# A four-layer attention and FFN kernel: weights folded inside the first chunk, first maxima inside the last one, and another arrangement of banks in the attention loop

## The reference

```python
scores = jnp.einsum('bhtd,bhtjd->bhtj', q, k_mod) * scale + pos_bias.T[None, :, None, :]
attn = jax.nn.softmax(jnp.where(valid[None, None], scores, jnp.finfo(scores.dtype).min), axis=-1)
out = jnp.einsum('bhtj,bhtjd->bhtd', attn, v_g) * if_gain[None, :, None, None]
...
h1 = jnp.einsum('gmh,goh->gmo', xg, W1) + b1[:, None, :]
h2 = jnp.einsum('gmo,gho->gmh', h1, W2) + b2[:, None, :]
...
attn = jax.nn.softmax(jnp.einsum('bqhd,bkhd->bhqk', q, k) * scale, axis=-1)
out = jnp.einsum('bhqk,bkhd->bqhd', attn, v)
```

## Time and profile before

| | |
|---|---|
| median of 3 runs | 2613.07 us (2612.34 to 2616.65) |
| profiled execution, its own time | 2615.01 us |
| its span, first to last instruction | 2613.2 us |
| PE busy | 2406.7 us (92%) |
| DVE busy | 2038.7 us (78%) |
| ACT busy | 1468.8 us (56%) |
| POOL busy | 727.3 us (28%) |
| granted PE clock, mean | 0.957 |

### The profile page before, as it was taken

One profiled execution on the slowest core, in us unless ns is written; L12 is line 12 of the kernel. 1 busy time (PEld: TensorE's weight loads), 2 busy tenths in 40 slices (PEclk: granted clock), 3 DMA queues, 4 the chain that ended last, 5 costly groups with the idle time before them and its releaser, 6 DMA issues. The chain is left out here.

```text
span 2613.2 us, 49018 instructions
## 1 busy us (share of the span) xinstructions
PE 2406.7 (92%) x15112; PEld 939.8 (36%) x15112; DVE 2038.7 (78%) x2445; ACT 1468.8 (56%) x2704; POOL 727.3 (28%) x936
## 2 busy tenths in 40 slices
PE   9688999999997648999999999999999999999678
PEld 7234455455445302323333333333333333333144
DVE  5388999999996348888888888888888888888145
ACT  0133444444434104777777777777777777777610
POOL 0688787787773033002002011020000000000110
PEclk9789999999998757999999999999999999999989
DMA  8334444554455197004004013031000000000161
GB/s 286 97 80 112 117 132 125 142 137 114 121 139 147 56 156 85 6 10 59 4 11 61 3 30 41 3 52 19 4 19 4 10 11 4 11 12 3 44 166 40
DMA packets 244668, 174.70 MB, mean 67 GB/s; under 512 B 105804, under 2 KB 215508, under 8 KB 244564
## 3 DMA queue, kind: packets, MB, share of 16 engines
q1 hardware_dynamic: 213048, 116.06, 16.9%
q0 software_dynamic: 13216, 36.72, 9.4%
q10 hardware_dynamic: 18304, 20.59, 2.7%
HBM read 116.49 MB, written 48.05 MB: 63 GB/s over the span
## 5 line engine op out<-in xcount | busy, mean ns | idle before, releaser
L1167 DVE TENSOR_REDUCE mx<-ps_m 128x1 f32<-128x1024 f32 x1036 | 1219.9, 1219 | 253.2 <-PE ps_m L1043 246.7
L1151 ACT ACTIVATE pr<-ps_s 128x512 f32<-128x512 f32 x2048 | 1114.9, 598 | 409.8 <-PE ps_s L1072 385.4
L1072 PE MATMUL ps_s<-qs,ks 99*128 (+1 forms) x2048 | 702.3, 382 | 9.9 <-ACT pr L1151 4.3
L1043 PE MATMUL ps_m<-ks,qs 96*128 (+1 forms) x2072 | 637.7, 389 | 39.9 <-DMA qs<-q_d 33.5
L1081 PE MATMUL ps_o<-pr,vg 128*32 128x512 f32 x4096 | 545.5, 605 | 0.2
L564 POOL TENSOR_TENSOR prod_p<-qT,kT 128x512 f32<-128x512 f32 x336 | 414.0, 1262 | 106.4 <-PE PSa L607 85.4
L1072 PEld LDWEIGHTS ps_s<-qs,ks 99*128 (+1 forms) x2048 | 195.8, 96 | 641.9 <-issue 441.0
L1000 POOL DMA_DIRECT2D vg<-vb_d x24 | 19.8, 824 | 1166.9 <-PE ps_o L1081 1166.5
L1043 PEld LDWEIGHTS ps_m<-ks,qs 96*128 (+1 forms) x2072 | 198.4, 98 | 252.3 <-issue 44.5
L815 DVE TENSOR_TENSOR prod_d<-PSa,kT 128x512 f32<-128x512 f32 x368 | 232.8, 678 | 25.0 <-PE PSa L607 15.5
L607 PE MATMUL PSa<-prod_p,sj 128*32 128x512 f32 x672 | 202.8, 617 | 10.0 <-DVE prod_d L815 7.5
(11 more groups left out here) (134 smaller groups left out, 2090.4 us busy)
## 6 DMA issues: line engine op xcount, KB each, us to landing
own<-skew SPq DMA_DIRECT2D x64, 512.0 KB
ks<-k_d POOLq DMA_DIRECT2D x42, 256.0 KB, 9.2
qs<-q_d POOLq DMA_DIRECT2D x168, 64.0 KB, 9.4
skew<-attn SPq DMA_DIRECT2D x64, 164.0 KB, 4.2
w<-in_W SPq DMA_DIRECT2D x32, 256.0 KB, 4.7
w<-in_W2T SPq DMA_DIRECT2D x32, 256.0 KB, 6.1
vb_d<-vb SPq DMA_DIRECT2D x8, 1024.0 KB, 5.3
q_d<-qparts ACTq DMA_DIRECT2D x16, 384.0 KB, 2.6
```

Of the source, the lines that this page charges most:

```text
L1043: mm = pe.matmul(ps_m[:, u % 2, kc * CH:(kc + 1) * CH], qs[0:KROWS, bass.ds(nq, 1), j, qt * P:(qt + 1) * P].rearrange("p a t -> p (a t)"), ...
L1072: pe.matmul(ps_s[:, op % SB, :], ks[:, bass.ds(slot, 1), j, kt * P:(kt + 1) * P].rearrange("p a t -> p (a t)"), qs[:, bass.ds(q, 1), j, :] ...
L1151: act.activation(pr[:, kt % 4, j, :], ps_s[:, op % SB, :], ACT.Exp, scale=HD ** -0.5).then_inc(p_ready, 1)
L1167: dve.tensor_reduce(mx[:, j * TILES + qt, half:half + 1], ps_m[:, u % 2, :], AX_X, ALU.max).then_inc(m_read, 1)
```

## The change

The change has three parts.

1. `fold_ffn` is gone. Its 32 pieces become steps `fold_load`, `fold` and `fold_out` of chunk 0 in the local stage, in a ring of four buffers, with the same matmuls and accumulation steps. One result buffer takes the place of two, and a second small matmul adds `b2`. The constants are loaded by ScalarE's queue.
2. The tensors of the full attention (`ks`, `qs` and others) are allocated ahead of both stages, and the local stage's big tensors are views of them. In chunk 7, behind the last product, GpSimd's queue loads the first keys and the queries of two chunks (18 transfers, `ahead_load`), and PE and VectorE make 88 maxima over 512 columns each (`ahead`), 64 for the first query chunk and 24 for the second. The attention's first pass of this kind is gone; at its start SP loads the queries of chunks 2 and 3.
3. In the attention loop the scores have four banks, the maxima three of one bank each; a `max_unit` is one matmul and a reduction over 512 columns, behind each score; values are made for two tiles at a time, once in eight scores. The transposed negative maxima use a maxima bank.

Beside these, the softmax of the local stage is made otherwise: the maximum's negative is the bias of eight exponentials on ScalarE, which also give the sums; the mask is added only for the first three tiles of a batch; the gain goes into `wo` once. `LEAD`, by which products are moved ahead, is 0.5 instead of 1.0, and the tables of positions are new.

```diff
+    (5.12, "fold_load", 19), (5.87, "fold_load", 20), (6.3, "fold_load", 21), (7.11, "fold_load", 22), (7.26, "load_v96", 0),
...
+            def fold(i):
+                g, r = i // PIECES, i % FOLD_RING
+                need(pe, fold_sb, g)
+                pe.wait_ge(fold_ld[r], 32 * (i // FOLD_RING + 1))
+                for m in range(KC):
+                    for k in range(FOLD_K):
+                        mm = pe.matmul(PS[:, TAIL_BANK[m], 0:C], fold_w[:, r, 0, k, m * P:(m + 1) * P], fold_w[:, r, 1, k, :],
+                                       start=(i % PIECES == 0 and k == 0), stop=(i % PIECES == PIECES - 1 and k == FOLD_K - 1))
+                mm.then_inc(piece_used, 1)
...
+            def ahead(u):
+                x, head, tile, kc = ahead_place(u)
+                if u == 0:
+                    pe.wait_ge(ahead_ld, 16 * 18)
...
+                need(pe, ahead_read, u - 2)
+                pe.matmul(PS[:, AHEAD_BANKS[u % 3], :], qs[0:KROWS, x, head, tile * P:(tile + 1) * P],
+                          ks[0:KROWS, 0, head, kc * CH:(kc + 1) * CH], start=True, stop=True).then_inc(ahead_ps, 1)
...
-                    act.activation(attn[:, w % 2, :, :], lg[:, :, :], ACT.Exp).then_inc(exp_ready, 1)
+                    for h in range(8):
+                        ex = act.activation(attn[:, w % 2, h, :], logits[:, h, :], ACT.Exp, bias=red[:, w % 2, 0, h:h + 1],
+                                            accum_out=red[:, w % 2, 1, h:h + 1])
+                    ex.then_inc(exp_ready, 1)
...
+            def max_bank_free(x, op):
+
+                read = x * MAX_OPS + (op - MB + 1 if op >= MB else (-1, 0, -2)[op])
+                pe.wait_ge(m_read, read)
+
+            def max_unit(x, e, nq, nslot):
+
+                op = max_op(e)
+                max_bank_free(x, op)
+                j, qt, kc = unit_place((CARRY + e) % MAXU)
+                pe.matmul(ps_m[:, op % MB, :], qs[0:KROWS, bass.ds(nq, 1), j, qt * P:(qt + 1) * P].rearrange("p a t -> p (a t)"),
+                          ks[0:KROWS, bass.ds(nslot, 1), j, kc * CH:(kc + 1) * CH].rearrange("p a t -> p (a t)"),
+                          start=True, stop=True).then_inc(m_ps, 1)
...
+                    for i in range(PER_PAIR):
+                        score(x, PER_PAIR * d + i, q, slot)
+                        e = PER_PAIR * d + i
+                        if sets and e == ROWS_AT:
+                            max_rows(x)
+                        if sets:
+                            max_unit(x, e, *sets[ahead])
...
+                    for kt in (2 * d - 2, 2 * d - 1):
+                        weigh(kt % KT, (x - 1) * SCORES + PER_PAIR * d)
```

More of the change, by code:

```diff
@@ L296, in order_of @@
+ONCE = {"fold_load": 0, "fold": 0, "fold_out": 0, "gain": 0, "ahead_load": NG - 1, "ahead": NG - 1, "ahead_rows": NG - 1}
+PIECES = 4
+FOLD_K = INTER // P // PIECES
+FOLD_RING = 4
+AHEAD_Q = GRP * TILES * NCH
+AHEAD_MAX = AHEAD_Q + AHEAD_Q * 6 // 16
+AHEAD_RUNS = [range(n, n + 2) for n in range(0, AHEAD_MAX, 2)]
 def order_of(steps, lead=0):
     at = [(SLOTS * j + s - lead, j, "products", s) for j in range(NG) for s in range(SLOTS)]
-    at += [(SLOTS * j + pos, j, what, i) for pos, what, i in steps for j in range(NG)]
+    at += [(SLOTS * j + pos, j, what, i) for pos, what, i in steps for j in range(NG) if ONCE.get(what, j) == j]
@@ new lines, in local_stage @@
+        fold_room = qs[:, 0:2, :, :].rearrange("p n j t -> p (n j t)").bitcast(F32)
+        mt = fold_room[:, 0:512].rearrange("p (k n) -> p k n", k=KC)
+        acc = fold_room[:, 512:768]
+        bc = fold_room[0:1, 768:1024]
+        b2s = fold_room[0:NG, 1024:1280]
+        b1s = fold_room[:, 1280:1344].rearrange("p (g k) -> p g k", g=NG)
+        column = fold_room[:, 1344:1345]
+        fold_ld = [sem("fold_ld" + str(n)) for n in range(FOLD_RING)]
+        bias_ld, piece_used, acc_step, fold_ps, fold_sb, fold_stored, late_ld = (
+            sem(n) for n in ("bias_ld", "piece_used", "acc_step", "fold_ps", "fold_sb", "fold_stored", "late_ld"))
@@ L450, in _ @@
         def _(sp):
-            def const(dst, src):
-                sp.dma_start(dst, src).then_inc(const_ld, 16)
             def load_head(j):
@@ L623, in step @@
                 w, c, tile = j * UNITS + i, i // 4, j * TILES + i % 4
-                if what == "h_mean":
+                if what == "fold":
+                    fold(i)
+                elif what == "fold_out":
+                    fold_bias(i)
+                elif what == "ahead":
+                    for u in AHEAD_RUNS[i]:
+                        ahead(u)
+                elif what == "ahead_rows":
+                    pe.wait_ge(nm_step, 5)
+                    pe.wait_ge(ahead_read, AHEAD_MAX)
+                    pe.transpose(PS[:, SC_BANK, 0:P // 2].bitcast(BF16), nmp[:, :, :].rearrange("p s n -> p (s n)"), identb[:, :]).then_inc(nmt_ps, 1)
+                elif what == "h_mean":
                     pe.wait_ge(head_ld, 16 * j + 16)
@@ L1032, in _ @@
         def _(pe):
-            pe.wait_ge(const_ld, 16)
-            pe.wait_ge(filled, 1)
-            def max_unit(u, taken, nq, nslot):
-                if not isinstance(taken, int) or taken >= 2:
-                    pe.wait_ge(m_read, taken - 1)
-                j, qt, half = unit_place(u)
-                for kc in range(2):
-                    c0 = (2 * half + kc) * CH
-                    mm = pe.matmul(ps_m[:, u % 2, kc * CH:(kc + 1) * CH],
-                                   qs[0:KROWS, bass.ds(nq, 1), j, qt * P:(qt + 1) * P].rearrange("p a t -> p (a t)"),
-                                   ks[0:KROWS, bass.ds(nslot, 1), j, c0:c0 + CH].rearrange("p a t -> p (a t)"),
-                                   start=True, stop=True)
-                mm.then_inc(m_ps, 1)
```

662 lines of the change are left out of this document (345 added, 317 removed).

## The result

The changed kernel took 2643.14 us (median of 4 runs, 2636.41 to 2645.48), the kernel before 2614.86 us on the same chip (4 runs, 2612.34 to 2618.66). The ratio is 1.0103, with a 95% interval of 1.0079 to 1.0126: slower by 28 us, where I had forecast no change. The range of 2560 to 2655 holds it. The profiled execution has a span of 2640.0 us, against 2613.2 before, so the traces differ by 26.8 us.

The account below looks back on a forecast made before the run. PE was taken to bound the loop, busy 1418.5 of 1420.5 us. The terms -28 - 9 + 13 - 64 + 89 - 1 sum to 0, so 2615 us, or 2613 as a median; range 2560 to 2655.

Parts of the forecast that it names:

- the two signs by which it was to be wrong: 512-column reads in the loop not 0.60 to 0.62 us apart, or chunk 0's products ending past 155 us.
- Fold merged: Start of the local stage: with the fold inside chunk 0, its products end at 140 instead of 167.7 us, -28 us.
- Softmax: Local stage chunks: work leaves VectorE, and a third of PE's idle time goes, 1.5 us over six chunks, -9 us.
- at most some 1.5 us more a unit: Local softmax: ScalarE's extra time for eight exponentials of 44 columns instead of one of 352, covered by its idle time.
- First maxima in the last outputs: Tail of chunk 7: 88 half-size maxima overfill VectorE and delay chain steps, +13 us (0 to +30).
- The 5 us: Tail of chunk 7: PE gives 5 us back, as maxima keep it busy where float32 matmuls ran partly at half clock.
- Wait for loads at the attention's start: Attention's start to first score: 82.5 us become 18, waiting for 12 query loads and a row of ones, -64 us.
- The loop: Full attention: three maxima banks hold PE in bursts of eight; pair 5.99 us, iteration 48.7 against 45.82, +89 us.
- Banks that don't hold PE: Loop: three maxima banks suffice or VectorE reads faster, iteration 44.5 us, kernel 2484 us; chance 0.09.
- A fold that starves: Chunk 0: accumulation steps wait long for GpSimd, four at 7.5 us each, 30 us come back, 2643 us; chance 0.07.
- Short reads that cost more: Loop: fixed cost of 0.125 us a read, pair 6.25 us, iteration 50.9, 70 us more, 2683 us; chance 0.07.
- The estimate of 0.66 us: Loop maxima: the skill table's time for a 512-column PSUM read, where the forecast took a pitch of 0.605 us.

## Why the prediction was wrong

The forecast of no change rested on gains and losses that cancel (four gains and two losses, not one as it says), so an error of 25 us in one term was enough. None of its three rivals, and neither of the two signs by which it was to be wrong, touches that term. The errors by stage are +3 for the fold, +11 for the softmax, +25 for the first maxima, -18 for the wait behind them, +4 for the loop and +1 at the end. That the total stayed in the range owes 18 us to a misreading: that part is luck.

- **Fold merged: right.** -24.7 against -28. The first product came at 50.2, not 45: VectorE's first accumulation step waited until 15.5 for the biases, and PE 4.9 us for ScalarE's square of the centred input. The products then lasted 92.8 us (forecast 95).
- **Softmax: wrong, though small.** I let a third of PE's idle time go, for -9. It was +2.1, and the run with the old softmax shows that neither VectorE's 12 us a chunk nor ScalarE's 14 more touch PE's pace beyond the scatter of 8 us from run to run. The shorter `LEAD` and the new positions, which stand in the same stage, no run takes apart from it. PE's 4.2 us of idle time in a chunk were the bound, and nothing spoke for a third of it. The step that said ScalarE gets "at most some 1.5 us more a unit" missed eight accumulator reads; it gets 2.1, which the slack hid.
- **First maxima in the last outputs: the step that failed.** I had +13 (0 to +30); it was +38. I added VectorE's busy time, found 10 us too much, added 8 for chain steps behind maxima, and took off 5 that PE was to give back by a higher clock. The busy time itself was right (88 reads of 0.62 us, 54.8 in the page's sum). What failed is the subtraction of VectorE's idle time from it, as if that time were free. Taking out 42 us of reading gave back 25.7, where I had priced all 53 us of it at 10 and the steps behind it at 8. My reading of this is that the idle time lay in a chain of steps in which each engine waits for the last, so that reads put into it delay the chain; the part that comes by PE's clock is not separated. The 5 us did not come: the clock was 0.77 against 0.80 before. Another 6 us come from the loads, which make PE wait with other work queued behind it; I had them land at nearly the right distance (25 us from the last product, they took 29), but did not ask what stands behind the wait. If the two add up, some 7 are left, for which I have no experiment; the reads over 8 columns still cost 12.5 us of VectorE's time.
- **Wait for loads at the attention's start: wrong, in the kernel's favour.** I had 18 us from the block's start to the first score; it was 0.4. The wait for the query loads stands in the sixth pair of the first iteration, not ahead of the first score. That is misread code, 18 us.
- **The loop: right.** Iteration 48.52 against 48.7, pair 5.96 against 5.99, and the kernel with four maxima banks shows the cause: 2.4 us of the iteration go. In the stage's +92.1, 8 us are the late row of negated maxima, which I did not foresee; without them the term is 84 against 88. Beyond eight equal pairs I had 0.4 and 0.3 us; it is 0.83, all in the pair with the transposed rows. With single tiles some 1.7 us lie beyond the tiles.
- **The rivals.** Banks that don't hold PE: out, by the trace and by two experiments. A fold that starves: out, 1.5 us at most. Short reads that cost more, 0.125 us each: out; the pitch is 0.60 to 0.61. The estimate of 0.66 us for 512 columns from PSUM, worked out from the table in the Trainium skill (VectorE: DVE Perf Modes, "The TRN2 errata — SBUF-src ops pay a fixed extra latency per instruction"), lies between this pitch and the 0.68 of one read alone. It is near the duration, and is not the pitch that the loop runs by.

The tail's term rested on a subtraction that no row bounded from above; its interval should have reached to the whole of the reading time, 53 us.

## What to carry to other kernels

Work moved into an engine's idle time is free only if that time is slack; where engines wait for each other in turn, ask for each insertion what stands behind it, and count the idle time as taken until a run shows otherwise. Splitting a read in two changes how many results a producer may run ahead by: compare the longest burst with the banks, not the mean rates, and batching the consumer's other work (values by pairs) makes that burst longer. Here the front of the change and the old loop, with the query loads early and one group's loads gated, give 2543 us, 2.9% under the kernel before.

## What the runs showed of the hardware

- A sum taken along with a ScalarE activation is a second instruction: 0.22 us on average for one column, behind an exponential of 44 columns of 0.31; one head after the other at a pitch of 0.32 us.
- A DMA of 12 KB from SyncE's queue, issued 11.3 us after the first of thirty loads of 64 and 256 KB from GpSimd's, had its first packet 11.2 us after its issue and its last after 17.3, and PE went on 19.7 us after the issue. Issued 8.3 us after the first load, its packets ran 9.0 to 10.0 us after the issue; with the loads gated away, 1.4 to 1.7. What sets the delay stays open.
- The releaser that a row names can be wrong: the 5.67 us put down to GpSimd's signal for a group went away by moving another group's loads.
- VectorE's operations with two inputs from SBUF, beside a busy GpSimd, took 0.39 to 1.50 us over 56 steps; the 8.23 us of the earlier trace rows were not met again, and what made them stays open.
